# Keys and values made once per sequence, with two ways of using a part of the TensorE array

## The reference

```python
x = x + xattn0(layernorm(x), ctx)     # 16 heads of 16, 77 keys from ctx (192 wide)
x = x + ffn0(layernorm(x))            # only expert 0 counts: layernorm(t + relu(t@w1+b1)@w2+b2)*gamma+beta, t its input
x = x + xattn1(layernorm(x), ctx)     # one head of 256
x = x + ffn1(layernorm(x))            # each row through the one of 8 matrices that its position picks

# xattn0
q = x @ w_q + b_q;  k = ctx @ w_k + b_k;  v = ctx @ w_v + b_v      # then 16 heads of 16
out = softmax(q k^T / 4) v @ w_o + b_o
```

## Time and profile before

| | |
|---|---|
| median of 3 runs | 337.02 us (335.79 to 338.06) |
| the profiled execution | 334.75 us, its span 332.7 us |
| PE busy | 288.5 us (87%), 1940 matmuls |
| DVE busy | 272.8 us (82%), 700 instructions |
| ACT busy | 200.7 us (60%) |
| POOL busy | 171.4 us (52%) |
| mean granted clock of PE | 0.952 of 2.4 GHz |
| chain that ended last | DVE 46%, PE 28%, issue 11%, ACT 7%, POOL 4% |

### The profile page before, as it was taken

The page is one execution under the profiler, slowest core; times in us unless marked ns, Lnnn a source line. Parts: engine busy times, 40 slices in busy tenths (PEclk is TensorE's granted clock), DMA queues, the critical chain, the costliest instruction groups (busy, mean ns, idle before and its releaser), DMA issues.

```text
span 332.7 us, 6124 instructions
## 1 busy us (share of the span) xinstructions
PE 288.5 (87%) x1940; PEld 264.4 (79%) x1940; DVE 272.8 (82%) x700; ACT 200.7 (60%) x655; POOL 171.4 (52%) x167
## 2 busy tenths in 40 slices
PE   3687897999996969989989999999999997996870
PEld 3576797999995869778968998998999896965650
DVE  2999999969988999999999589579977889675750
ACT  4649759385743289568857695985767365164320
POOL 2372530343596845523680373249889375316744
PEclk9956799999997999999999999999999998999995
DMA  6812101100115710000000000000310000001212
GB/s 181 306 44 87 28 26 49 40 31 2 42 56 205 206 33 2 1 2 32 2 1 3 32 0 2 0 18 19 95 32 2 1 3 0 2 1 48 80 47 79
DMA packets 8796, 15.30 MB, mean 46 GB/s; under 512 B 1270, under 2 KB 6813, under 8 KB 8509
## 3 DMA queue, kind: packets, MB, share of 16 engines
q1 hardware_dynamic: 6845, 9.68, 8.9%
q0 software_dynamic: 1920, 5.25, 5.6%
HBM read 11.77 MB, written 3.15 MB: 45 GB/s over the span
## 4 chain that ended last, share of the span: by engine, by line
DVE 46%; PE 28%; issue 11%; ACT 7%; POOL 4%; DVEq 1%; DMA 1%; SPq 0%; POOLq 0%; ACTq 0%
PE PB L254 13%; PE PB L247 7%; DVE SX L624 5%; DVE SM L570 4%; PE PB L434 4%; ACT E L1052 3%; DVE XN L591 2%; DVE XTL L597 2%; DVE HH L657 2%; POOL out_x L1283 2%; PE S L357 2%; DVE XTL L607 2%; DVE XTH L607 2%; DVE KBL L755 2%; DVE SM L573 1%
## 5 line engine op out<-in xcount | busy, mean ns | idle before, releaser
L1212 POOL TENSOR_TENSOR SM<-SM,nhalf 128x2 f32<-128x2 f32 x40 | 29.5, 738 | 63.8 <-DVE SM L576 60.0
L1052 ACT ACTIVATE E<-S,SX 128x77 f32<-128x77 f32 x128 | 39.5, 335 | 24.1 <-DVE SX L627 23.8
L1246 POOL TENSOR_TENSOR HL<-HF,HH 128x512 fp32r<-128x512 f32 x26 | 34.7, 1345 | 19.5 <-DVE HH L657 19.4
L254 PE MATMUL PB<-W2H,HH 128*128 128x256 f32 x128 | 38.9, 304 | 3.1 <-DVE HL L663 2.3
L254 PE MATMUL PB<-XTH,W1H 128*128 128x256 f32 x128 | 37.5, 293 | 1.8 <-DVE XTL L597 1.8
L247 PE MATMUL PB<-ET,VB 124*128 124x256 f32 x160 | 36.9, 380 | 0.0
L254 PE MATMUL PB<-W2L,HH 128*128 128x256 f32 x128 | 36.4, 284 | 0.0
L254 PE MATMUL PB<-W2H,HL 128*128 128x256 f32 x128 | 36.4, 284 | 0.0
L254 PE MATMUL PB<-XTH,W1L 128*128 128x256 f32 x128 | 36.2, 283 | 0.0
L254 PE MATMUL PB<-XTL,W1H 128*128 128x256 f32 x128 | 36.2, 283 | 0.0
L1018 ACT ACTIVATE XN<-X,SM 128x256 f32<-128x256 f32 x32 | 19.3, 605 | 23.6 <-DVE SM L581 23.5
(11 more groups left out here) (195 smaller groups left out, 877.7 us busy)
## 6 DMA issues: line engine op xcount, KB each, us to landing
RAW<-in_w SPq DMA_DIRECT2D x4, 512.0 KB, 5.8
WD<-in_WD SPq DMA_DIRECT2D x2, 1024.0 KB, 7.6
X<-in_x SPq DMA_DIRECT2D x4, 256.0 KB, 7.8
x<-X SPq DMA_DIRECT2D x4, 256.0 KB, 2.5
bc<-in_rows SPq DMA_DIRECT2D x1, 768.0 KB, 7.5
RAW<-in_w_q SPq DMA_DIRECT2D x1, 256.0 KB, 4.1
Wo<-in_w_o SPq DMA_DIRECT2D x1, 256.0 KB, 8.0
RAW<-in_WqT SPq DMA_DIRECT2D x1, 256.0 KB, 2.8
```

The costliest lines, as they stand in the source:

```text
L254: t = e.matmul(dst, a, b, start=first and j == 0, stop=last and j == n - 1)
L1052: t = e.activation(Ei[:, h * NK:(h + 1) * NK], P[:, at:at + NK], ACT.Exp, bias=SX[:, i, 2, k:k + 1], accum_out=SX[:, i, 1, k:k + 1])
L1212: e.tensor_tensor(sm(K, g, 9), sm(K, g, 8), nhalf[:, :], ALU.pow).then_inc(s["rs" + K], 1)
L1246: e.tensor_tensor(HL[:, hs, :], HF[:, (4 * g + j) % 3, :, :], f(HH[:, hs, :]), ALU.subtract).then_inc(s["hlP"], 1)
```

## The change

Keys: `keys` makes both sequences at once (154 columns), `kf` adds the bias for both in two full instructions, and KBH and KBL hold both sequences, each feature on its own partition and nowhere else. So the 64 features of bank `u` are 64 partitions, and `sc` becomes six matmuls over 64 partitions each, high by high, high by low, low by high, in turn on the lower and the upper 64 partitions. `qh` and `ql` are two instructions of 128 partitions instead of four of 64.

Values: `vmat` makes the values of both sequences once (77 rows), `vs` adds the bias, `vrep` repeats them over the chunk's 124 rows by a matmul with `REP` (identities side by side, written by `rep`), only for the heads that a chunk holds, all chunks of a sequence in one bank, and `vb` masks them out of that bank. `cr` is gone. Both sequences are done near the start. `pv(g, a)` becomes eight matmuls that give 32 features each: for every 32 output partitions the two chunks that hold their heads.

End of the feed-forward block: `apply("Y")`, x2P and x2D are replaced by `x2` on DVE, four instructions of 128x256 per group: (Y - mean) * gamma ahead of the wait for `rs`, then times the factor plus X.

All five lists are written out in a new order.

```diff
-        KBH = sb("KBH", [128, 16, NK], F32R)
-        VB = sb("VB", [CW, 5, 2, 128])
+        KBH = sb("KBH", [128, 2, 8, NK], F32R)
+        VB = sb("VB", [CW, 2, 512])
...
+        REP = XTE[0:NK, 1, 0:5 * CW]
+        VS = XP[0:NK, 0, :, :]
+        def pairs_of(c):
+            first, n = max(c - 1, 0), 1 if c in (0, 4) else 2
+            return first, n, (0, 64, 192, 320, 448)[c]
...
+            def vrep(b, p):
...
+                for c in range(5):
+                    first, n, at = pairs_of(c)
+                    t = full(P[0:CW, at:at + 64 * n],
+                             [(REP[:, c * CW:(c + 1) * CW],
+                               VS[:, b, :].rearrange("p (a n) -> p a n", a=2)[:, :, 32 * first:32 * (first + n)])])
...
             def sc(g, i, a, k):
...
-                for u in range(2):
-                    h = 8 * a + 4 * u
-                    kh, kl = (T[:, h:h + 4, :].rearrange("p h k -> p (h k)") for T in (KBH, KBL))
-                    Q = (XTH, XTL)[u][:, 1 + g % 2, a, ts]
-                    t = full(P[:, u * 512:u * 512 + 4 * NK], [(Q, kh), (Q, kl)])
+                for j, (Q, KB) in enumerate(((XTH, KBH), (XTH, KBL), (XTL, KBH))):
+                    for u in range(2):
+                        own = slice(64 * u, 64 * u + 64)
+                        t = e.matmul(P[:, u * 512:u * 512 + 4 * NK], Q[own, 1 + g % 2, a, ts],
+                                     KB[own, b, 4 * a:4 * a + 4, :].rearrange("p h k -> p (h k)"),
+                                     start=j == 0, stop=j == 2)
...
             def pv(g, a, p):
...
-                full(P[:, a * 256:(a + 1) * 256],
-                     [(VB[:, c, a, :], ET[:, g % 2, a, c, :]) for c in range(5)]).then_inc(s["pv"], 1)
+                for c in range(2):
+                    for n in range(4):
+                        first, m, at = pairs_of(n + c)
+                        at += 32 * (a * m + n - first)
+                        t = e.matmul(P[32 * n:32 * n + 32, a * 256:(a + 1) * 256], VB[:, g // 4, at:at + 32],
+                                     ET[:, g % 2, a, n + c, :], start=c == 0, stop=c == 1)
...
             def ql(g):
...
+                    e.scalar_tensor_tensor(out=XTL[:, 1 + g % 2, m, :], in0=P[:, m * 256:(m + 1) * 256],
+                                           scalar=col("b_q", m), in1=f(XTH[:, 1 + g % 2, m, :]),
+                                           op0=ALU.add, op1=ALU.subtract).then_inc(s["ql"], 1)
...
+            def x2(g):
+                Y = dst_of("Y", g)
+                for i in range(2):
+                    step(e.scalar_tensor_tensor(out=Y[:, i, :], in0=Y[:, i, :], scalar=smi("Y", g, i, 6, 7),
+                                                in1=bc[:, GAMMA, :], op0=ALU.subtract, op1=ALU.mult))
+                settle()
+                w.wait_ge(s["rsY"], g + 1)
+                w.wait_ge(s["be"], g + 1)
+                for i in range(2):
+                    e.scalar_tensor_tensor(out=X[:, g, i, :], in0=Y[:, i, :], scalar=smi("Y", g, i, 9, 10),
+                                           in1=X[:, g, i, :], op0=ALU.mult, op1=ALU.add).then_inc(s["x2"], 1)
...
-            keys(0, 0); tA(0, 1); vals(0, 0, 2); vals(0, 1, 3); vals(0, 2, 0); q(0, 1); vals(0, 3, 2); vals(0, 4, 3)
+            keys(0); tA(0, 1); vmat(2); q(0, 3); vrep(0, 0); vrep(1, 1); sc(0, 0, 0, 0); sc(0, 0, 1, 1); r_scores(2)
```

More of the change, by code:

```diff
@@ L212, in x2_here @@
         def x2_here(w, g):
[L213 to L216, removed]
+            w.wait_ge(s["x2"], 2 * g + 2)
         def hl_here(w, g, j):
@@ L565, in stats @@
                     x3_here(w, g)
-                if g > 1:
+                if g > 1 and K == "Y":
+                    x2_here(w, g - 2)
+                elif g > 1:
                     w.wait_ge(s["bi" + K], g - 1)
@@ L751, in kbl @@
             def kbl(b):
                 settle()
-                w.wait_ge(s["kf"], 2 * b + 2)
-                for m in range(4):
-                    t = e.tensor_tensor(KBL[:, 4 * m:4 * m + 4, :], KF[:, m, :].unsqueeze(1).to_broadcast([128, 4, NK]),
+                for m in range(2):
+                    t = e.tensor_tensor(KBL[:, b, 4 * m:4 * m + 4, :],
+                                        KF[:, m, b, :].unsqueeze(1).to_broadcast([128, 4, NK]),
                                         mask4[:, :].unsqueeze(2).to_broadcast([128, 4, NK]), ALU.mult)
-                    t.then_inc(s["kbl"], 1) if m == 3 else step(t)
@@ L759, in vb, with vs @@
-            def vb(b, c):
-                n = 5 * b + c
-                w.wait_ge(s["p_v"], n + 1)
+                    t.then_inc(s["kbl"], 1) if m else step(t)
+            def vs():
+                w.wait_ge(s["p_v"], 1)
                 w.wait_ge(s["bc"], 16)
+                e.tensor_tensor(VS, two(bank("vmat")[0:NK, :]), bc[0:NK, BV, :].unsqueeze(1).to_broadcast([NK, 2, 256]),
+                                ALU.add).then_inc(s["vs"], 1)
+            def vb(b):
+                w.wait_ge(s["p_v"], b + 2)
@@ L1034, in qh @@
                 for m in range(2):
-                    for u in range(2):
-                        own = slice(64 * u, 64 * u + 64)
-                        Q = (XTH, XTL)[u][:, 1 + g % 2, m, :]
-                        e.activation(Q[own, :], P[own, m * 256:(m + 1) * 256], ACT.Identity,
-                                     bias=col("b_q", m)[own, :]).then_inc(s["qh"], 1)
+                    e.activation(XTH[:, 1 + g % 2, m, :], P[:, m * 256:(m + 1) * 256], ACT.Identity,
+                                 bias=col("b_q", m)).then_inc(s["qh"], 1)
             def ex(g, i, a):
@@ L1247, in hlP @@
                                 ALU.subtract).then_inc(s["hlP"], 1)
-            def x2P(g):
-                Y = dst_of("Y", g)
-                w.wait_ge(s["apY"], g + 1)
-                w.wait_ge(s["biY"], g + 1)
-                w.wait_ge(s["be"], g + 1)
-                e.tensor_tensor(Y, Y, rows(GAMMA), ALU.mult).then_inc(s["gam"], 1)
-                w.wait_ge(s["gam"], sum(not late(a) for a in range(g + 1)))
-                e.tensor_tensor(X[:, g, :, :], Y, X[:, g, :, :], ALU.add).then_inc(s["x2P"], 1)
             def sx(g):
```

357 lines of the change are left out of this document (164 added, 193 removed).

## The result

The kernel after takes 314.81 us (median of 4 runs, 314.18 to 315.8) against 337.37 us of the kernel before beside it: ratio 0.934, 95% interval 0.9297 to 0.9383. The forecast of 327 us had the sign right and less than half of the 22.6 us. The profiled execution took 315.8 us, its span 314.0 us.

A forecast was written before the change was run, and what follows sets the result against it. DVE and PE were taken to bound 30 to 180 us, PE alone 180 to 270, latency the end. Start -2, middle -8, PE's stretch +2.2, end -2 make -9.8 from 337.0: 327 us, 8-in-10 range 314 to 341.

The forecast's parts named there:

- two thirds of 11.9: Middle, 30 to 180 us: DVE loses 11.9 us of work, of which two thirds, -8 us, shorten the time.
- leaves other waits, or finds more than I count: Rival on the new order: the relief is not used, or more is found; 320 to 345 us, chance 0.08.
- `pv` at 1.94 us: PE: a `pv` call in column strips takes 1.94 us instead of 2.16, -0.22 per call.
- The rival of four strips at once: PE's `pv`: four column strips always run together, 0.86 us a call, about 317.5 us in all; chance 0.20.
- one after the other: Rival for PE's `pv`: strips do not overlap, 3.46 us a call, about 344 us in all; chance 0.14.
- the nine steps: PE's `pv`: a strip's second record runs beside the next strip's first, giving 9 x 0.216 = 1.94 us.
- `sc` at 0.66 us: PE: six weight loads of 0.11 us limit an `sc` call to 0.66 us, +0.09 per call.
- Switches at 0.10 us: PE: about 71 changes between split and whole array cost 0.10 us each, bounds 0.05 and 0.35.
- `x2` at 0.45 us: DVE: each 128x256 instruction of `x2` takes 0.45 us, 14.4 us for eight groups of four.
- DVE's total of 255 us: DVE's whole busy time falls from 272.8 to 255 us.
- Start, -2 us: Up to the first scores: halved DVE work against added early work gives -2 us, bounds -4 and +1.
- End, -2 us: From Y's sum to C's statistics, group 7: about -1.6 us; with some for group 6, -2 us.

The follow-up runs named there:

- the ninth profile: Kernel after with each list in the new order up to y of group 2, the remaining calls in the old order: 324.75 us, ratio 0.9698.

## Why the prediction was right or wrong

- **What bounds the kernel: wrong, and the cause of the miss.** "From 30 to 180 us a microsecond off DVE is worth part of a microsecond", two thirds of 11.9. In the old order the work came off (DVE 139.4 to 129.2 us from 30 to 180, PE 136.4 to 128.0 in that same kernel) and the time fell 3 us in all. DVE's share of 93% was not a bound; the lists met each other too late, and what the relief freed became idle time on both.
- **The order counted as nothing: wrong.** The sum had no term for it. It measures about 3.4% with the old forms and 5.4 to 5.7% with the new ones, 11 us alone and 18 to 19 with the new forms. The rival that the order "leaves other waits, or finds more than I count" had 0.08, spread over 320 to 345 us. It was the case, and the time lies below its spread.
- **`pv` at 1.94 us: wrong, measured 1.00.** The rival of four strips at once had 0.86; the rest is the switch and the longer step to the second four. "If records start in order, and the two of a strip can't share it" is the premise that failed: the sixteen records run four at a time, and a call takes the same time with the four of a strip in a row. Against 16 x 0.216 = 3.46 us for one after the other it is a factor of 3.5. The Trainium skill (TensorE: Matmul & The Clock Gate, Part 3) has 2.38 for three strips; the sum that the prediction made from it, 1.15 us, was nearer than its own 1.94. The strict order of start on that page, from which the nine steps came, does not fit the 1.02 us with the four of a strip in a row, and the measurement decides. The rival's time of 317.5 us was near the result partly by chance: put back in the new order, the wide `pv` costs 3.8% beside the new `sc` and 0.9% beside the old one, and the 6.5 + 3 us that the rival counted lie between these.
- **`sc` at 0.66 us: size off.** Pairs start together, 0.14 us apart (0.25 from the first to the second), so the loads, which the forecast took as the limit, do not set this pace. Alone a call takes 0.63 us with the switch behind it, against 0.57 before and 0.66 plus switches forecast.
- **Switches at 0.10 us: about right.** The loads show 0.17 to 0.19 us idle, PE's starts 0.08 us beyond the pace (five transposes of 0.11 from 150.43, `pv` at 151.06) and 0.09 (the last pair of `sc` at 152.45 plus 0.15, the next matmul at 152.69). PE's whole busy time was forecast near 288 and is 267.9: 16 x (1.94 - 1.00) = 15 us of the 20 are `pv`.
- **`x2` at 0.45 us: right for most, too low in the mean.** 0.48 us by the median, but 0.72 and 0.54 in the mean, from the five that run beside POOL; the forecast had no term for that. `x2` takes 18.7 us, not 14.4. DVE's total of 255 us was met (254.8) partly by luck: `ql` takes 6.8 us instead of 7.7 and KBL 1.7 instead of 2.7. Alone in the old order `x2` costs 4.2 us; the forecast had +3.1 in the middle and a gain at the end.
- **Start, -2 us: right for the scores, wrong for what follows.** First scores at 16.80 us (19 forecast, 21.14 in the earlier trace rows), but y(0) 8.4 us later. The step looked at DVE and PE alone. With the row of gathers broken up y(0) comes at 84.7 us, so most of the loss is the stall beside that row.
- **End, -2 us: wrong.** From Y's sum to C's statistics of group 7 are 6.4 us, not 5.2 (6.8 before); behind it the tail is 3.2 us longer (40.7 against 37.5). Why the tail grew, no run here was made to show; the old order with the full new work has it too (46.9 us from y(7) to the end, 44.3 before).

These two rows are the first scores and, on DVE, C's statistics of group 7, after:

```profile
16.80 0.41 PE L365 MATMUL S<-KBH,XTH 64*128 64x308 f32 x2
```

```profile
266.88 0.68 DVE L695 TENSOR_TENSOR XN<-PB,XN 128x512 f32<-128x512 f32 x1
...
273.28 0.74 DVE L598 BATCH_NORM_STATS2 SM<-X 128x6 f32<-128x256 f32 x2
```

## What to carry to other kernels

In a program whose engines run fixed lists, a busy share of 93% does not make an engine the bound: taking 10 us off it, and 8 off the next one, gave 3 us of 337 until the lists were written anew, so a change of prices and a change of order have to be weighed as one. A change that rewrites all lists has a term of its own, which may be larger than every price; bound it from the idle time of all engines in the slices of the old profile, not from the waits of one engine. And look in the new lists for rows of gathers that stood apart before, and in the trace for signals that come late beside them: spreading four calls was worth 3 to 4 us here, though one kernel had the row and no stall.

## What the hardware showed beyond that

- Plain float32 matmuls of 32 columns of weights on four column strips: sixteen records of 256 columns in 1.00 us at 2.4 GHz, switch included, four starting within 0.02 us of one another, in both orders of the list that ran (1.00 and 1.02 us); ten whole-array ones take 2.16.
- float32r matmuls on the two row halves start together, 0.14 us a pair of 308 columns.
- Eight indirect DMAs in a row on POOL, 10 us: in eight of nine profiles a semaphore raised by PE's matmuls goes up 2.7 us or more behind their end beside them. In the kernel after ACT and PE wait for it, and PE idles 4.35 us of 20 at a granted clock of 0.83. With the eight in pairs it does not, and in the ninth profile the signals are in time beside the same row.
- `scalar_tensor_tensor` on DVE, 128x256 float32 from SBUF: 0.48 us by the median, 1.35 to 1.52 us in the five of 32 that run beside an elementwise instruction of POOL for over 1 us.
